# The first attention of a fused AdaLN block in f16 halves, with turned scores, in one run over its four batches

## The reference

```
mod = silu(c) @ wmod                       # six rows of 128 per batch: sa, ca, ga, sb, cb, gb
h = layernorm(x) * (1 + ca) + sa
q, k, v = split(h @ w_qkv.T)               # one head of 128
p = softmax(q @ k.T / sqrt(8))             # 1024 x 1024 per batch
o = (p @ v).T reshaped to 1024 x 128       # features and tokens exchanged, then read in rows
x = x + ga * (o @ w_proj.T + b_proj)
h = layernorm(x) * (1 + cb) + sb
x = x + gb * ffn(h)   # rmsnorm, causal attention with rotated heads, rmsnorm, 8 experts
```

## Time and profile before

| what | us |
|---|---|
| median of 3 runs (lowest to highest) | 1386.56 (1386.06 to 1386.67) |
| the profiled execution, its own time | 1383.45 |
| its span, first to last instruction | 1381.3 |
| start to the first scores of batch 0 | 48.9 |
| batches 0, 1, 2, 3 of the first attention (scores to scores, the last to its last row of x1) | 50.7, 53.4, 54.1, 42.4 |
| from there to the first scores of round 0 | 55.0 |
| the 16 rounds, routing and experts | 1076.8 |

### The profile page before, as it was taken

The page is one execution under the profiler, slowest core; times in us unless marked ns, Lnnn a source line. Parts: engine busy times, 40 slices in busy tenths (PEclk is TensorE's granted clock), DMA queues, the critical chain, the costliest instruction groups (busy, mean ns, idle before and its releaser), DMA issues.

```text
span 1381.3 us, 33911 instructions
## 1 busy us (share of the span) xinstructions
PE 1153.0 (83%) x13948; PEld 840.3 (61%) x13948; DVE 1044.2 (76%) x2139; ACT 791.6 (57%) x1438; POOL 977.5 (71%) x772
## 2 busy tenths in 40 slices
PE   2789889569999999999999999999999998600881
PEld 1467566326676676776676767767767676500871
DVE  4448556568889888888898898888988975592666
ACT  1333434128877777787787877877877886100220
POOL 4234562748988898898888988988988897326355
PEclk7899999769999999999999999999999999655996
DMA  9300002031221222121221211212212110022793
GB/s 234 96 16 16 31 0 82 24 91 42 56 74 37 57 57 56 51 59 45 68 47 52 74 36 51 59 55 58 52 47 48 36 25 2 1 68 87 210 286 142
DMA packets 49232, 90.70 MB, mean 66 GB/s; under 512 B 8768, under 2 KB 19136, under 8 KB 48832
## 3 DMA queue, kind: packets, MB, share of 16 engines
q1 hardware_dynamic: 46128, 81.27, 21.0%
q0 software_dynamic: 2960, 7.38, 2.1%
HBM read 44.02 MB, written 13.01 MB: 41 GB/s over the span
## 4 chain that ended last, share of the span: by engine, by line
PE 67%; DVE 15%; DMA 6%; POOL 5%; issue 4%; ACT 2%; SPq 1%; POOLq 0%; DVEq 0%
PE psT L995 5%; PE psS L1065 5%; PE psS L1064 5%; PE psT L983 5%; PE psS L1086 5%; PE psS L1087 5%; PE psS L1088 4%; PE psO L945 4%; DMA rows_out<-arena,back 3%; PE psS L933 3%; PE psO L995 3%; PE psT L1013 3%; PE psO L1065 3%; PE psO L1064 3%; POOL rows_in L697 2%
## 5 line engine op out<-in xcount | busy, mean ns | idle before, releaser
L671 POOL TENSOR_TENSOR probs<-arena,probs 128x512 f16<-128x512 f32 x576 | 652.9, 1159 | 122.7 <-ACT probs L804 122.4
L804 ACT ACTIVATE probs<-arena 128x512 f16<-128x512 f32 x576 | 357.9, 622 | 0.0
L812 ACT ACTIVATE arena<-psS 128x512 f32<-128x512 f32 x384 | 228.0, 594 | 148.6 <-PE psS L1068 82.6
L1086 PE MATMUL psS<-vb,probs 128*128 128x65 f16 x2304 | 302.0, 192 | 4.6 <-POOL probs L671 2.4
L1087 PE MATMUL psS<-vb,probs 128*128 128x64 f16 x2304 | 303.3, 194 | 0.0
L1088 PE MATMUL psS<-vb,probs 128*128 128x65 f16 x2304 | 301.3, 192 | 0.0
L1086 PEld LDWEIGHTS psS<-vb,probs 128*128 128x128 f16 x2304 | 220.1, 97 | 72.8 <-issue 9.4
L1087 PEld LDWEIGHTS psS<-vb,probs 128*128 128x128 f16 x2304 | 215.5, 97 | 47.4
L1416 DVE TENSOR_REDUCE pmax<-psT 128x1 f32<-128x512 f32 (+1 forms) x305 | 193.7, 640 | 35.3 <-PE psT L998 17.7
L1088 PEld LDWEIGHTS psS<-vb,probs 128*128 128x128 f16 x2304 | 216.8, 98 | 0.0
L1416 DVE TENSOR_REDUCE pmax<-psO 128x1 f32<-128x512 f32 (+1 forms) x207 | 139.3, 673 | 30.4 <-PE psO L995 23.7
(11 more groups left out here) (242 smaller groups left out, 2537.6 us busy)
## 6 DMA issues: line engine op xcount, KB each, us to landing
arena<-arena SPq DMA_DIRECT2D x240, 128.0 KB, 2.3
arena<-w_exp_dram SPq DMA_DIRECT2D x40, 384.0 KB, 4.2
arena<-xnT_d SPq DMA_DIRECT2D x16, 512.0 KB, 3.5
wkv<-w_d SPq DMA_DIRECT2D x16, 352.0 KB, 4.1
arena<-x_dram SPq DMA_DIRECT2D x8, 512.0 KB, 3.7
rows_in<-arena POOLq DMA_DIRECT2D x1, 2580.0 KB, 26.7
arena<-rows_in SPq DMA_DIRECT2D x40, 64.5 KB, 3.3
xnT_d<-arena SPq DMA_DIRECT2D x4, 512.0 KB, 2.6
```

Of the source, the lines that this page charges most:

```text
L671: pool.tensor_tensor(pl[:, r, :], pf[:, r, :], ph[:, r, :], ALU.subtract).then_inc(lo_P, 1)
L804: act.activation(ph[:, s % RING, :], pf[:, s % RING, :], ACT.Copy).then_inc(b_hi, 1)
L812: act.activation(pf[:, s % RING, :], score_banks[s % SCORES], ACT.Exp).then_inc(b_exp, 1)
L1086: pe.matmul(dst, high, vb[:, p, j, 0:OW], start=first, stop=False, skip_group_check=True)
```

## The change

The scores are made turned: keys lie on the partitions, queries along the row, so the probabilities come out as the values' matmul wants them, and the transposes and their copies go. The row maximum must then be known before the scores: PE first makes the tile's scores from the high halves alone, unturned (`side_task` "max"), DVE takes their maximum (`row_max`) and writes it on a diagonal in f16 (`diag`), and a matmul of ones with that diagonal subtracts it inside the scores' sum. Query, key, values, normalised input, weights, probabilities and the attention's output are each held as a high f16 half and a low one; each product is three f16 matmuls instead of one f32 one. The values have a column of ones, whose product is the row sum. The work of the next batch (`part`: turned input, queries, keys, values) is put into tiles 3 to 6 of a batch, so that tiles run on from batch to batch. All sides (`part`, `max`, and the turning `in2`) use one PSUM buffer, `psTf`, one after the other. Squares move from POOL to ACT; POOL makes the low half of every tile's probabilities. The modulation of the first input is done by ACT on the turned input, that by g1 in the copy of input2. SP loads x in two forms again: in order of columns into two buffers, and in rows straight into `hres`. Loops that were loops are written out (t runs over 32 tiles, `NL`).

The core of the diff ("..." where lines are left out):

```diff
+def side_of(t):
+    b, i = divmod(t, NT)
+    before = [("part", b + 1, i - 3)] if 3 <= i < 7 and b + 1 < B else []
+    if t == 3 * NT - 5 + 8:
+        before.append(("in2", 0))
+    return before, [("max", t + 2)] if t + 2 < NL else []
+FIRST_SIDE = [("part", 0, k) for k in range(4)] + [("max", 0), ("max", 1)]
+SIDE_L = FIRST_SIDE + [e for t in range(NL) for part in side_of(t) for e in part] + [("in2", 1)]
...
+            sp.dma_start(cs[:, :], cT).then_inc(const_in, 16)
             load_nat(0)
+            sp.dma_start(cst[:, :], consts).then_inc(const_in, 16)
+            sp.dma_start(wm, wmod).then_inc(wm_in, 16)
+            sp.dma_start(wqkv[:, :], w_qkvT).then_inc(qw_in, 16)
+            sp.dma_start(wproj[:, :], w_projT).then_inc(qw_in, 16)
+            load_nat(1)
+            sp.dma_start(wraw, w_kv.rearrange("h p n -> p h n")).then_inc(wraw_in, 16)
+            sp.dma_start(woraw, w_o.rearrange("h p n -> p h n")).then_inc(wo_in, 16)
...
+            sp.wait_ge(w_lo, HKV)
             sp.dma_start(w_d.rearrange("h p a n -> p h a n"), wsplit).then_inc(w_out, 16)
+            sp.wait_ge(w_out, 16)
             for b in range(B):
+                sp.dma_start(hres[:, b, :, :], x[b].rearrange("(p j) e -> p j e", p=P)).then_inc(xrow_in, 16)
+            for b in range(2, B):
+                sp.wait_ge(n1_V, N1V * (b - 2) + 3)
+                load_nat(b)
+            store_input2(0)
+            sp.wait_ge(xn_out, 16)
+            for it in range(2):
+                load_round(it, it)
+            store_input2(1)
...
+            def with_rows(c):
+                xb = x1[:, c, :, :]
+                pool.wait_ge(n2_P, c + 1)
+                pool.wait_ge(xrow_in, 16 * B)
+                pool.tensor_tensor(xb, xb, hres[:, c, :, :], ALU.add).then_inc(xsum, 1)
...
+            for t in range(NL):
+                b, i = divmod(t, NT)
+                pool.wait_ge(a_ph, t + 1)
+                pool.tensor_tensor(pl0[:, t % 3, :], pf0[:, t % 3, :], ph0[:, t % 3, :], ALU.subtract).then_inc(a_pl, 1)
+                if 3 <= t < 3 + HKV:
+                    pool.wait_ge(w_hi, 1)
+                    pool.tensor_tensor(wsplit[:, t - 3, 1, :], wraw[:, t - 3, :], wsplit[:, t - 3, 0, :], ALU.subtract
+                                       ).then_inc(w_lo, 1)
+                if t == 3:
+                    pool.wait_ge(fill_ready, 1)
+                    pool.dma_start(rows_in.rearrange("(t p) d -> p t d", p=P), empty).then_inc(zero_in, 16)
...
+                if i == 1 and 1 <= b and b + 1 < B:
+                    norm1_power(b + 1)
+                if i == 1 and b >= 3:
+                    norm2_power(b - 3, 1)
+                if i == 2 and b >= 2:
+                    norm2_power(b - 2, 0)
+                if i == 3 and b >= 1:
+                    gated(b - 1)
+                if i == 4 and b >= 3:
+                    input2_low(b - 3)
...
+            norm2_power(1, 1)
+            norm2_power(2, 0)
+            gated(3)
+            pool.wait_ge(ones_set, 4)
+            input2_low(1)
+            norm2_power(3, 0)
+            norm2_power(2, 1)
+            shifted(3)
             low_half(2, 0, 0)
...
+            def part_high(c, k):
+                act.wait_ge(a_side, SIDE_END["part", c, k])
+                r = c % 2
+                if k == HT:
+                    act.wait_ge(mod_Tc, 2)
+                    act.activation(psTf, psTf, ACT.Identity, scale=ca1T[:, c:c + 1], bias=saT[:, c:c + 1]).then_inc(in_mod, 1)
+                    act.wait_ge(in_mod, c + 1)
+                    act.activation(hT[:, 0, :], psTf, ACT.Copy).then_inc(a_hi, 1)
...
+            for t in range(NL):
+                b, i = divmod(t, NT)
+                r = t % 3
+                act.wait_ge(a_S, t + 1)
+                if t >= 3:
+                    act.wait_ge(a_pl, t - 2)
+                act.activation(pf0[:, r, :], psS[:, t % 2, :], ACT.Exp, scale=A_SCALE).then_inc(a_E, 1)
+                act.wait_ge(a_E, t + 1)
+                if t >= 3:
+                    act.wait_ge(a_PV, t - 2)
+                act.activation(ph0[:, r, :], pf0[:, r, :], ACT.Copy).then_inc(a_ph, 1)
+                if t == 2:
+                    act.wait_ge(wraw_in, 16)
+                    act.activation(wsplit[:, :, 0, :], wraw, ACT.Copy).then_inc(w_hi, 1)
+                if t == 3:
+                    act.wait_ge(wo_in, 16)
+                    act.activation(wo16[:, :, 0, :], woraw, ACT.Copy).then_inc(wo_hi, 1)
+                if 3 <= i < 7 and b + 1 < B:
+                    part_high(b + 1, i - 3)
+                if i == 7 and b + 2 < B:
+                    norm1_squares(b + 2)
+                if i == 7 and b >= 1:
+                    norm2_squares(b - 1, 0)
+                if i == 7 and b >= 2:
+                    norm2_squares(b - 2, 1)
+                if i == 2 and b >= 3:
+                    norm2_out(b - 3)
+                if i == 3 and b >= 3:
+                    input2(b - 3, psTf)
...
+            norm2_out(1)
+            input2(1, psTf)
+            high_half(0, 0, 0, VEC_PRO[ROTATED[0]])
+            norm2_squares(3, 0)
+            norm2_squares(2, 1)
+            high_half(1, 0, 0, VEC_PRO[ROTATED[1]])
+            norm2_out(2)
+            norm2_squares(3, 1)
+            high_half(2, 0, 0, VEC_PRO[ROTATED[2]])
...
+            def side_task(n):
+                if n > 0:
+                    prev = SIDE_L[n - 1]
+                    if prev[0] == "max":
+                        pe.wait_ge(a_top, prev[1] + 1)
+                    elif prev[0] == "part":
+                        pe.wait_ge(a_lo, 4 * prev[1] + prev[2] + 1)
+                    else:
+                        pe.wait_ge(n2_T, prev[1] + 1)
+                e = SIDE_L[n]
+                if e[0] == "in2":
+                    turn_input2(e[1], psTf)
+                    return
+                if e[0] == "max":
+                    b, i = divmod(e[1], NT)
+                    pe.wait_ge(a_hi, 4 * b + KL + 1)
+                    for h in range(2):
+                        mm = pe.matmul(psTf[:, h * 512:(h + 1) * 512], ql0[:, b % 2, 0, i * P:(i + 1) * P],
+                                       kl0[:, b % 2, 0, h * 512:(h + 1) * 512], start=True, stop=True)
+                    mm.then_inc(a_side, 1)
+                    return
...
+                if k == HT:
+                    pe.wait_ge(n1_V, N1V * (c + 1))
+                    for j in range(NT):
+                        mm = pe.transpose(psTf[:, j * P:(j + 1) * P], n1[:, j, :], ident)
...
+            def scoresA(t):
+                b, i = divmod(t, NT)
+                r = b % 2
+                if i == 0:
+                    pe.wait_ge(a_lo, 4 * b + KL + 1)
+                pe.wait_ge(a_dg, t + 1)
+                if t >= 2:
+                    pe.wait_ge(a_E, t - 1)
+                at = slice(i * P, (i + 1) * P)
                 for j in range(NT):
...
+            def valuesA(t):
+                pe.wait_ge(a_pl, t + 1)
+                if t >= 2:
+                    pe.wait_ge(a_x1, t - 1)
...
+                    high, low = ph0[:, t % 3, j * P:(j + 1) * P], pl0[:, t % 3, j * P:(j + 1) * P]
+                    pe.matmul(dst, high, vl0[:, r, j, 0:D + 1], start=(j == 0), stop=False, skip_group_check=True)
+                    pe.matmul(dst[:, 0:D], high, vl0[:, r, j, D + 2:VL], start=False, stop=False, skip_group_check=True)
+                    mm = pe.matmul(dst, low, vl0[:, r, j, 0:D + 1], start=False, stop=(j == NT - 1), skip_group_check=True)
+                mm.then_inc(a_PV, 1)
...
+            for t in range(NL):
+                before, after = side_of(t)
+                scoresA(t)
+                for e in before:
+                    side_task(SIDE_AT[e])
+                if t >= 2:
+                    valuesA(t - 2)
+                for e in after:
+                    side_task(SIDE_AT[e])
+                if t >= 3:
+                    projA(t - 3)
+            valuesA(NL - 2)
+            projA(NL - 3)
+            valuesA(NL - 1)
+            side_task(SIDE_AT["in2", 1])
+            projA(NL - 2)
+            projA(NL - 1)
...
             for i in range(len(PROLOGUE)):
+                if i == 0:
+                    pe.wait_ge(n2_T, 2)
+                    pe.wait_ge(a_x1, NL)
+                    pe.wait_ge(late_in, 16 * NLATE)
                 if PROLOGUE[i] == ("max", G, 0):
+                    turn_input2(2, psS[:, 0, :])
+                    pe.wait_ge(ones_set, 4)
+                if PROLOGUE[i] == ("max", G + 1, 0):
+                    turn_input2(3, psS[:, 1, :])
...
+            def norm1_a(c):
+                v.wait_ge(xnat_in[c % 2], 16 * (c // 2) + 16)
+                if c > 0:
+                    v.wait_ge(a_side, SIDE_END["part", c - 1, HT])
+                centred(n1_V, N1V, c, x_nat[c % 2], n1, st1, 0)
+                centred(n1_V, N1V, c, x_nat[c % 2], n1, st1, 1)
...
+            def part_low(c, k):
```

(127 more changed lines are left out.)

596 lines of the change are left out of this document (226 added, 370 removed).

## The result

The changed kernel took 1409.62 us (median, 1402.34 to 1410.83), the kernel before 1386.62 (1386.06 to 1389.21): ratio 1.0153, interval 1.013 to 1.0176, slower. The profiled execution of the changed kernel has a span of 1407.9 us, and round 0 starts at 326.87, where it started at 304.56: 22.3 later. From there to the end of the span it is 1081.0 here and 1076.7 before (1407.9 less 326.9, 1381.3 less 304.6), and 1078.2 in a second profile of the changed kernel: of the rest some us vary, and the 22.3 arise ahead of round 0, in the stages that the change touches.

The account below looks back on a forecast made before the run. TensorE bounds the kernel before; afterwards waits between engines would. 41.0 + 67.3 + 51.9 + 52.9 + 41.1 + 14.3 + 48.5 put round 0 at 317.0, 12.5 later: median 1399, own range 1389 to 1410, with rivals 1380 to 1420.

Parts of the forecast that it names:

- the late load: Batch 0, tile 5: VectorE waits for x of batch 2, queued on SP behind the weights' store; 17 us lost.
- the two rings: Waits per tile: plain, values wait for VectorE's x1 row, 4.7; part tile, one psTf buffer, 7.2 or 8.3 us.
- Start, 41.0: Kernel start to first scores: norm1, turned input, queries, keys, values and maxima; first scores at 41.0 against 48.9.
- Tile 6, 27: Batch 0, tile 6: ends 27 us after tile 5 because of the awaited load, instead of about 10.
- Rival (b): Batch 0, tile 5: x of batch 2 is already there; 17 us fall away, 1382; chance 0.08.
- The stops between VectorE and GpSimd, 0.2 to 0.4 a tile: First attention's tiles: the two engines block each other; 0.2 to 0.4 us per plain tile, up to 1.7 in some.
- Batch 3 to the last row, 55.4: Last batch without parts, 41.1 us, then last row of x1 14.3 after the last tile.
- The drain, 48.5: Last row of x1 to round 0: GpSimd's queue is the chain, 14 operations of 33; 48.5 us against 55.0.
- Rival (a): Drain shrinks to batch 3's bare chain, 30 us instead of 48.5; time 1380; chance 0.14.
- Rival (c): TensorE's clock falls in part tiles, each of the 12 costing 1.75 us; 1420; chance 0.09.
- Rival (d): TensorE's f16 matmuls start farther apart in longer streams, 0.083 instead of 0.055 us; 1423; chance 0.05.
- Rival (e): Whole kernel: gains at start and drain and the late load cancel, no change, 1386; chance 0.06.

## Why the prediction was right, step by step

The direction and the main steps held: the late load, the two rings, GpSimd's queue in the drain. The size was short: round 0 shifted by 22.3 where 12.5 were forecast. The median lies 0.4 inside the end of the range, 1410, and that much is luck; the second run of the change gave 1405.03.

**Start, 41.0: the first scores were issued at 36.9, 4.1 earlier.** The matmul groups of queries, keys and values took 1.5 each, at a granted clock of 1.00, where 1.3 to 2.6 were put. At the scores TensorE was granted 0.50 of full speed, the 1.2 GHz level, so they took until 40.5, and the first exponential, from which the batches here are counted, began at 40.55. That it falls beside 41.0 is luck: an early start and slow scores cancel.

**Batch 0, 67.3: took 69.7. Tile 6, 27: took 29.5.** The load came late by the chain of waits that was written out, and the early load gave back 16.4 in this batch, where 17 was put. The tile without the wait was put at 10 and takes 13.5, with a step of the gates in it. Rival (b) is out: VectorE did wait, 15.9.

**Batches 1 and 2, 51.9 and 52.9: took 50.7 and 53.2.** The plain tile was 4.8 (4.7 without a stop was put), the part tile 6.9 (7.2), by the two rings that were named; turning each ring's order shortened it (3.8 and, with both, 6.2). That the sums fit is in part two errors that cancel: batch 1's four plain tiles took 19.7 instead of 21.6, and `HT` was mis-sized, 10.0 and 9.8 instead of 8.3: its transposes wait for `norm1_c`, which stands behind x1 in VectorE's queue. TensorE's timeline:

```profile
127.22 1.81 PE L950 MATMUL psT<-cst,arena 128*128 128x128 f32 x8 [2.02 <-DVE arena L1347]
```

**The stops between VectorE and GpSimd, 0.2 to 0.4 a tile: the diagonal lost 0.3 on average** (0.555 less 0.25), but not tile by tile: most in batches 1 and 2 lost nothing, and eight tiles lost 0.5 to 1.9 each. Halving the subtraction and moving the diagonal gave 7.3 and 11.4, of which batch 3 may owe some to its spread. It fits the Trainium skill, "SBUF — State Buffer", section "Who interferes with whom": VectorE and GpSimd share a pair of ports under an exclusive lock, and ScalarE never waits. The trace agrees: ScalarE's 0.40 is the same each time, and so is VectorE's 0.351 from PSUM, while its passes with two operands in SBUF are stretched, from 1.23 to 3.10 in the centring shown above, as before the change.

**Batch 3 to the last row, 55.4: took 58.0 and 55.6.** So the second large loss was forecast, tail and all. GpSimd's gate, sum and scaling stand between its subtractions there. The spread was not forecast, and TensorE's clock goes with it (0.84 and 0.94). In the slower profile it fell behind a wait for VectorE's row of x1, and the values and the maximum ran at about the half level:

```profile
226.13 0.22 PE L1000 MATMUL psO<-arena,probs 128*128 128x129 f16 x1 [1.92 <-DVE x L1407]
```
```profile
226.40:229.90 3.50, 3.50 (x32) 2.95 (x29) 2.47 (x3) 2.45 (x8) 3.38 (x3) 0.52 0.00 0
```

**The drain, 48.5: took 54.7.** This is the mis-sized term. GpSimd's timeline gives its parts:

```profile
272.36 1.64 POOL L563 TENSOR_TENSOR rstd2a<-st2a,cst 128x8 f32<-128x8 f32 x1 [5.59 <-DVE st2a L1329]
273.96 2.35 POOL L575 TENSOR_TENSOR x<-x,mod 128x1024 f32<-128x1024 f32 x1
276.38 3.20 POOL L582 TENSOR_TENSOR x<-x,hres 128x1024 f32<-128x1024 f32 x1
279.64 1.80 POOL L657 MEMSET arena<- 1x2048 f16 x1
...
293.00 1.65 POOL L563 TENSOR_TENSOR rstd2a<-st2a,cst 128x8 f32<-128x8 f32 x1 [4.63 <-DVE st2a L1329]
...
316.30 1.65 POOL L563 TENSOR_TENSOR rstd2b<-st2b,cst 128x8 f32<-128x8 f32 x1
```

Up to the power that ends at 317.95 GpSimd has 16 operations of 34.0 us (14 of 33 were put) and waits 11.5 (9.5 put for VectorE's and ScalarE's pieces). The stretch from there to round 0 took 8.9 instead of 6: `norm2_out` of batch 3 (L747) stands on ScalarE behind the row read (L845), which waits for VectorE's ten maxima, and the 8 transposes took 1.97 at the half level (0.50 granted) against 1.06 at 269.39.

```profile
319.50 0.27 ACT L845 ACTIVATE hrow<-psT 8x128 f16<-8x128 f32 x1 [5.36 <-PE psT L1078]
319.67 2.43 ACT L747 ACTIVATE arena<-hres,rstd2b 128x128 f32<-128x128 f32 x8
```

That GpSimd's queue is the chain was right: the row of ones moved within it gave 1.0, about what the sum beside it lost by being stopped (3.20 there, 2.34 with the edit). Rival (a) is out for the reason given, eight other operations between.

**Rival (c)** is out as it was put, 1.75 in each of 12 part tiles: the granted clock was 0.97 in batches 1 and 2, part tiles and all. But the clock did fall elsewhere: 0.50 in the late load (84 to 104), where TensorE stood, at the scores of tile 4 of batch 0 (59.05 to 62) behind a wait of 5.14, and in parts of the start, of batch 3 and of the drain, behind waits, as behind the gap of the earlier trace rows. **Rival (d)** is out. In tile 5 of batch 0 these are the first and the last of 32 score matmuls in TensorE's timeline, which answers to the earlier trace rows:

```profile
67.64 0.22 PE L982 MATMUL psS<-arena 128*128 128x128 f16 x1
...
69.37 0.22 PE L985 MATMUL psS<-arena,ones 128*128 128x128 f16 x1
```

They start 1.73 / 31 = 0.056 apart. The 81 ns of the Trainium skill, "TensorE: Matmul & The Clock Gate", "Back-to-back issue gap", aren't seen. **Rival (e)** is out by the interval.

**Other edits.** The squares took 1.04 to 1.06 and the Identity pass 1.17, about a copy's 1.02, and ScalarE loaded no table between its first one, at 0.72, and round 0: the term put at nothing was nothing.

What stays open is how the 11.4 of the moved diagonal divide between its 0.25 and the stops, and what makes batch 3 vary.

## What to carry to other kernels

When one engine's work per tile shrinks, write out the ring of waits through the in-order queues, and put in each queue first what the engine at the ring's head waits for: here the same instructions in another order were worth 35 us, where batches 1 and 2 saved 8 and 10 us of TensorE's work and became 3.7 and 0.4 shorter. A load needed soon doesn't belong behind a wait for another engine's last tile. Before trusting a gain of a few us read from one profile, see how much the same stretch differs between profiles of the same code: here 4.4 us in one batch. Small operations between SBUF operands that TensorE waits for go to ScalarE when GpSimd is busy.

## What the runs showed of the hardware

A 128x128 operation of VectorE took 0.25 us alone and 2.18 beside a GpSimd subtraction that began in the same 0.01 us; ScalarE's took 0.40 at all times. With TensorE at the half level, f16 matmuls of 128 columns start 0.106 apart (59.05, 59.16, 59.26), at full speed 0.056. GpSimd's subtraction of 512 columns took 1.27, of 1024 columns 2.22.
